# The three middle attention layers of a graph network as running sums by scans on VectorE, with rows gathered by position

## The reference, cut to what matters

```python
xs = (h @ Ws).reshape(N, H, C)
alpha_s = jnp.sum(xs * a_s, axis=-1);  alpha_d = jnp.sum(xd * a_d, axis=-1)
e = leaky_relu(alpha_s[src] + alpha_d[dst], 0.2)
ex = jnp.exp(e - segment_max(e, dst)[dst])
alpha = ex / (segment_sum(ex, dst)[dst] + 1e-16)
out = segment_sum(xs[src] * alpha[:, :, None], dst).reshape(N, H * C) + bias
```

## Time and profile before

| what | value |
|---|---|
| median of 3 runs | 10667.48 us (10661.7 to 10689.28) |
| the profiled execution's own time | 10696.05 us |
| its span, first to last instruction | 10694.3 us |
| PE / PEld / DVE busy | 5622.2 / 3714.7 / 4834.9 us |
| ACT / POOL busy | 1790.8 / 6522.5 us |
| gathers of the first network (912) | 426.4 to 1876.8 us of the span |
| gathers of the three middle layers (896 each) | 2068.0 to 3473.6, 3605.2 to 4999.7, 5107.8 to 6485.2 us |
| MLP over the edges, sum by source, end | about 6608 to 8610, 8896 to 10480, to 10694 us |

### The profile page before, as it was taken

One profiled execution on the slowest core, in us unless ns is written; L12 is line 12 of the kernel. 1 busy time (PEld: TensorE's weight loads), 2 busy tenths in 40 slices (PEclk: granted clock), 3 DMA queues, 4 the chain that ended last, 5 costly groups with the idle time before them and its releaser, 6 DMA issues. The chain is left out here.

```text
span 10694.3 us, 107517 instructions
## 1 busy us (share of the span) xinstructions
PE 5622.2 (53%) x22192; PEld 3714.7 (35%) x22192; DVE 4834.9 (45%) x11928; ACT 1790.8 (17%) x4846; POOL 6522.5 (61%) x6001
## 2 busy tenths in 40 slices
PE   6387878233333433334233334888888885333332
PEld 5133333133333333323233233444444443333332
DVE  6398989433332222222222223556565534444443
ACT  1211111211111100001000002333333331000002
POOL 2466666466666566665666665555555526888885
PEclk8688888566656556556555556999999986555555
DMA  1432324322223122222222223333333313444445
GB/s 67 120 59 56 58 56 56 78 44 46 43 45 45 38 44 46 45 45 41 45 45 46 46 46 69 88 86 91 89 92 85 90 30 31 36 36 36 36 36 95
DMA packets 705533, 611.82 MB, mean 57 GB/s; under 512 B 392917, under 2 KB 587604, under 8 KB 704308
## 3 DMA queue, kind: packets, MB, share of 16 engines
q0 software_dynamic: 332784, 513.58, 26.3%
q1 hardware_dynamic: 372676, 97.46, 4.3%
HBM read 483.12 MB, written 126.04 MB: 57 GB/s over the span
## 5 line engine op out<-in xcount | busy, mean ns | idle before, releaser
L899 POOL DMA_INDIRECT big<-table_layer,rec_L x2688 | 2658.9, 989 | 1598.8 <-issue 845.5
L970 PE MATMUL sums_L<-h,ident 128*128 128x128 f32 (+1 forms) x5376 | 1606.3, 465 | 720.7 <-DVE h L1068 301.9
L974 PE MATMUL sums_L<-carry_L,ident 128*128 128x128 f32 (+1 forms) x1792 | 679.5, 473 | 2172.6 <-DVE carry_L L1077 1438.6
L1077 DVE TENSOR_TENSOR carry_L<-sums_L,shrink_L 128x128 f32<-128x128 f32 (+1 forms) x896 | 348.1, 389 | 2841.9 <-remote 2222.7
L2061 POOL DMA_INDIRECT sums_by_source<-msg,to x896 | 1420.9, 1586 | 286.7 <-issue 227.6
L970 PEld LDWEIGHTS sums_L<-h,ident 128*128 128x128 f32 x5376 | 1092.2, 277 | 1200.3 <-issue 1175.0
L899 POOL DMA_INDIRECT big<-table_layer,idx_L x912 | 946.1, 1037 | 538.4 <-issue 307.2
L974 PEld LDWEIGHTS sums_L<-carry_L,ident 128*128 128x128 f32 x1792 | 395.2, 265 | 2359.7 <-DVE carry_L L1077 1497.4
L1611 POOL DMA_INDIRECT big<-table_layer,rec_m x900 | 859.2, 955 | 274.3 <-issue 274.3
L1661 PE MATMUL ps<-big,w 128*128 128x512 f32 x1792 | 833.5, 608 | 0.0
L924 ACT ACTIVATE big<-run_z_L 128x4 f32 (+1 forms) x900 | 194.6, 216 | 3554.4 <-DVE carry_L L1077 2257.0
(11 more groups left out here) (376 smaller groups left out, 8664.9 us busy)
## 6 DMA issues: line engine op xcount, KB each, us to landing
big<-table_layer,rec_L POOLq DMA_INDIRECT x2688
big<-table_layer,idx_L POOLq DMA_INDIRECT x912
table_layer<-xr SPq DMA_DIRECT2D x49, 296.0 KB
big<-table_layer,rec_m POOLq DMA_INDIRECT x900
sums_by_source<-msg,to POOLq DMA_INDIRECT x896
sums_by_source<-big SPq DMA_DIRECT2D x4, 3200.0 KB
q<-sums_by_source SPq DMA_DIRECT2D x28, 448.0 KB, 6.3
own_L<-own_layer SPq DMA_DIRECT2D x672, 2.0 KB
```

The costliest lines, as they stand in the source:

```text
L899: G.indirect_dma_start(out=g[b][:, u, s, :], out_offset=None, in_=table, in_offset=bass.IndirectOffsetOnAxis(ap=at, axis=0)).then_inc(gath ...
L970: PE.matmul(sums[b][u][:, 0:T * D], ident[:, :], prod[PROD[u]][:, s, :], start=(s == 0), stop=False, skip_group_check=True)
L974: PE.matmul(sums[b][u][:, 0:T * D], ident[:, :], carry[u % 2][:, :], start=False, stop=True, skip_group_check=True).then_inc(summed, 1)
L1077: V.tensor_tensor(carry[u % 2][:, :].rearrange("p (l c) -> p l c", c=C), before[:, 0:T * D].rearrange("p (l c) -> p l c", c=C), bc(shrink[ ...
```

## The change

- **Middle layers.** `attention` is used for the first network only. A new function `gat` does a middle layer. Its two buffers (`ring`, `RB` = 2) hold 16 slots each. A slot is an element of a running sum, with no items' sums and no PE: DVE makes the 4 products of a batch transposed (`prod`, channels outside, slots inside; the sources are read with a stride of 132 words), and then one scan over 4 x 33 x 17 = 2244 elements multiplies the running sum by `shrink` and adds `prod`. ACT expands the 64 fade values to 2112 with one exponential, and copies for each of the 4 items the element after its last slot into the accumulator.
- The own part of the score comes from PE: a one-hot of tile numbers against `own1T`, the transposed own scores, in place of SP's four small fetches.
- SP fetches for each batch the source positions (64 bytes a partition) and the tile numbers and lifts. It does so after the batch before in this buffer has been kept by ACT.
- **By position.** Tables hold rows by the node's place in the order. `onward` writes them with plain DMAs from SP, in place of POOL's scatters. The places are put into a spare column of the first network's table, come back with its gathers, and ACT and SP store them (`posb`, `pos_d`) for later layers and the MLP.
- Turns of the counting part are 26 in place of 25.

```diff
-            attention(f"L1{l}", 1, tab1_d[l], own1, acc1, g1, *scratch(1), ...)
+            gat(l, count if l == 0 else None)
```

Outside `gat`:

```diff
                         for j in range(NT):
-                            pool.wait_ge(staged, j + 1)
-                            G.indirect_dma_start(out=table, out_offset=... nid[:, j:j + 1] ..., in_=st[j % STG][:, 0:width])
+                            sp.wait_ge(staged, j + 1)
+                            sp.dma_start(table[j * P:(j + 1) * P, :], st[j % STG][:, 0:width]).then_inc(rows_out[j % STG], 16)
...
+                    if j >= EARLY:
+                        A.activation(stage[j % STG][:, :, A0], rank[:, j:j + 1].to_broadcast([P, T4]), ACT.Copy)
...
+                        act.wait_ge(pos_out[b], i * 16 + 16)
+                        A.activation(posb[b][:, :].rearrange("p (u s) -> p u s", s=S), g[b][:, :, :, A0], ACT.Copy
+                                     ).then_inc(pos_ok[b], 1)
...
+                        sp.dma_start(pos_d[:, ds((i * U + b * B) * S, B * S)], posb[b][:, :]).then_inc(pos_out[b], 16)
```

More of the change, by code:

```diff
@@ L34 @@
 HSTEP = 16
-HTURNS = 25
-EC2 = HTURNS * 2 * HSTEP
+RB = 2
+HTURNS = 26
+EC2 = HTURNS * RB * HSTEP
+SLOTS = B * S
 STG = 4
-PADI = 2 * U + U
+PADI = 48
 RMAX = 160
@@ L428, in _ @@
             def _(dve):
+                for v in range(STG):
+                    last = V.memset(stage[v][:, :, A0:A0P], 0.0)
+                last.then_inc(pos_blank, 1)
                 dve.wait_ge(edges_in, 16)
@@ L838, in attention @@
                 kept = sem(f"sums_kept_{tag}")
[L839 to L843, removed]
-                    counted = [sem(f"source_counted{b}") for b in range(2)]
-                    hist_ok = sem("sources_counted")
-                    histp = pb(f"histp_{tag}", [P, 512], fp32, ph)
                 NREC = 3 if T > 1 else 1
@@ L881, in _ @@
                         for b in range(2):
-                            fetch(i, b)
-                    if ahead:
-                        fetch(n, 0)
-                    if blank is not None:
-                        sp.wait_ge(zeroed, 16 * S)
+                            fetch(i + 1, b)
+                            store(i, b)
+                    for b in range(2):
+                        sp.wait_ge(own_in[b], n * 16 * B + 16 * B)
+                        sp.sem_inc(gate_s, 1)
+                        sp.wait_ge(pos_out[b], n * 16 + 16)
+                        sp.sem_inc(gate_s, 1)
                 @block.gpsimd
@@ L926, in keep @@
                                      ACT.Copy).then_inc(kept, 1)
+                    for b in range(2):
+                        act.sem_inc(pos_ok[b], 1)
                     act.sem_inc(kept, 2 * B)
@@ L956, in _, with turn @@
                 def _(pe):
[L957 removed]
+                    def turn(i):
                         for b in range(2):
@@ L962, in turn @@
                                 pe.wait_ge(kept, (i * 2 + b) * B + u + 2 + 2 * B - NB)
-                                if counting and u == 0:
-                                    pe.wait_ge(onehot[b], i + 1)
-                                    for t in range(HSTEP):
-                                        last = PE.matmul(histp[:, 0:NT], oneL[b][:, :, t], oneH[b][:, :, t],
-                                                         start=False, stop=False)
-                                    last.then_inc(counted[b], 1)
                                 for s in range(S):
@@ L978, in _ @@
                     n = turns(pe)
[L979 to L991 removed]
+                    with pe.Fori(0, n) as i:
+                        turn(i)
                 @block.vector
@@ L1544, in gnn @@
                 off = [sb(f"off{v}", [P, S], bf16, ph) for v in range(2)]
+                frm = [sb(f"from{u}", [P, S], i32, ph) for u in range(U)]
                 gx, ge, eT, h0, h1, h2, at = [], [], [], [], [[], []], [], 0
```

416 lines of the change are left out of this document (310 added, 106 removed).

## The result

| | before | changed | ratio, 95% interval |
|---|---|---|---|
| medians of 20 runs each | 10667.67 us | 10717.73 us | 1.0045 (1.0035 to 1.0054) |
| profiled execution, span | 10694.3 us | 10716.4 us | |

The changed kernel is slower by 50 us, 0.45%. The forecast was slower by 140 us. The sign and the likeliest mechanism were right.

A forecast was written before the change was run, and what follows sets the result against it. Middle layers were taken as bound by POOL's gather issue plus slow-sequencer waits. Loops +190, start -46, tables -17, preamble +8, first network +5 gave +140 us; less 28.6 for the profiled execution, 10808 us, 1.3% slower, range 10080 to 11130.

The forecast's parts named there:

- The gathers, products and the scan: Middle layers: bare gathers 20.0 us a batch, four products of 1.08 us each, one scan of 4.8 us.
- What DVE does to POOL: Middle layers: DVE instructions with two SBUF operands hold POOL, 4.2 us a batch for the scan, 1.3 for products.
- The chain that frees a buffer: Middle layers: last gather through keep and next fetch takes 22.2 us, covered by POOL's 25.5 us for the other batch.
- The crawl after the change: Middle layers: sequencers and semaphores slow during POOL's long gather bursts with register loads; 0.5 us a batch allowed.
- First middle layer's start: First middle layer: both first fetches stand ahead of SP's zeros, so gathers start earlier; gain 46 us.
- Tables by SP's plain DMAs: Between stages: SP writes four tables in place of POOL's scatters, PE and ACT needing nearly as much; net -17 us.
- The small terms: Outside the middle layers: preamble +8 us, first network +5, MLP 0.
- D: Rival, 0.10: in middle layers POOL's holds and its present waits cancel; 24.9 to 25.2 us a batch, 10640 to 10670 us.
- B: Rival, 0.31: the scan doesn't hold POOL in middle layers; 21.1 to 23.5 us a batch, 10052 to 10388 us.
- C: Rival, 0.17 with what lies above: slow register loads lengthen ACT's keep; 28.5 to 29 us a batch, 11228 to 11310 us.

The follow-up runs named there:

- shrink_psum: Changed kernel with shrink in PSUM, so the long scan has one SBUF operand instead of two; 10167.77 us, 0.9646 of before.
- ring_of_4: Changed kernel with RB = 4 in place of 2, and 13 counting turns of 4 batches in place of 26 of 2; 10626.74 us.
- set 3: Kernels run on one shared chip; the kernel before took 9521.85 us, the changed one 10259.81 us, ratio 1.0778.
- pool_scatters_2: Changed kernel with the four tables again written by POOL's indirect DMAs instead of SP's plain DMAs; 10865.97 us, 1.0148 of before.
- psum_weights_ring4_3: Changed kernel with shrink and a second copy of the weights in PSUM, and RB = 4; 0.9708 of before; the same kernel as psum_weights_ring4, there 0.9764.
- Sets 2 and 5: Two groups of runs: kernel before 9531.53 and 10559.04 us, changed kernel 1.0758 and 1.0099 of it.

## Where the prediction was right, and where it was wrong

*The gathers, products and the scan* were right. The products took 1.065 us (forecast 1.08), the scan 4.83 (4.8).

*What DVE does to POOL* was right in kind, and shrink_psum shows it by taking the second operand away. Its size was 5.7 us a batch against 5.5: some 4.3 us for the scan (forecast 4.2), 1.4 for the products and, in the first layer, the count's instructions (forecast 1.3 for the products alone). I let a gather ask at a random point of the scan. It doesn't: the gather beside the last product ends with it (2646.19 and 2646.34 us), so that in three of four batches the next one asks just after the scan has begun (0.06 us) and loses 4.57 us, and else 1.05 us into it and loses 3.60. That the mean of the two lies so near the mean of a random point is luck.

*The chain that frees a buffer* was rightly called covered (ring_of_4). *The crawl after the change*, 0.5 us a batch, was not there; 0.35 us of other pauses stood in its place. Small errors cancel: 26.0 forecast, 26.1 measured, +190 and +207 us.

*First middle layer's start*, -46 us, was right for the first gather (46.4), but I left out what is given back when POOL has used its 32 gathers and the third fetch is behind the zeros: I wrote that down, and didn't price it. Net some -33 to -36.

*Tables by SP's plain DMAs*, -17 us, is the step that failed. It priced the table between the first two middle layers by its one long scatter alone, and said that "in the other two PE and ACT need nearly as much" as the scatters. No row stood behind it. Between the stages the changed kernel gained 158.6 us, and 46.4 of them are the start; so the term is -112 us, not -17 (-99 by the traces of set 3). By table it is -16, -39, -38 and -19 where I had -5, -8, -1 and -3. ACT and PE stood waiting for POOL's scatters, and ran a tile in 0.71 us once SP wrote them. I had taken the waits of two engines in a chain for their work. The earlier trace rows could have told me: 49 scatters of 0.967 us with pauses of 0.30 are 62 us of the 70 that the third table took, and ACT had 29 us of work there. That the writer is the cause is shown by pool_scatters_2, which gives the scatters back to POOL in the changed kernel and takes 142 us more. This is some 30 us more than the whole term; the rest of what the change puts between the stages, such as the transposes of `own1`, would cost about that much the other way, and no run separates it.

The traces differ by +22 us where +140 was forecast. The tables make 95 us of these 118. The small terms (preamble, first network, MLP and what follows) were -26 together where I had +13, which makes 39; the loops give 17 the other way. In set 3 the two kernels' first networks and MLPs lie within 3.1 us of each other, so most of the -26 is the difference of two executions and no effect of the change. In the medians it is made up by the 28 us by which the trace of before lay over its own: 207 - 46 - 112 is +49, where the medians differ by 50.

Two smaller slips: the scatters' starts span 77.8 and 69.5 us in the second and third table, where I had 78.9 and 70.5 with the last scatter's own time; and D's 24.9 to 25.2 us a batch are 10622 to 10672 us by its own sum, not 10640 to 10670.

*Rivals.* B, the other side, gave 21.1 to 23.5 us a batch and 10052 to 10388 us if the scan doesn't hold POOL: shrink_psum built that case, with 23.0 to 23.6 us a batch and 0.9646 of before, which of the result's 10668 us would be 10290. C, the crawl on the serial chain, came only once the holds were gone (psum_weights_ring4_3). D's mechanism didn't happen, though the time ended not far from it.

*What the prediction didn't know* is that its baseline isn't one number. It took 4.9 us a batch of crawl in before as given. In sets 2 and 3 there is none, and the same change costs 7.6 and 7.8%: where the crawl is there, the holds that the change adds are largely paid for by the waits that it removes. So a forecast near the measured time is in part a matter of the set that it was measured in.

What stays open: what the crawl is, and why some sets have none. Sets 2 and 5 are recorded under the same chip number, one without it and one with it, so if that number names one chip, the chip alone doesn't decide. Why the changed kernel's loops never crawl is not known either; that POOL is stopped by a hold every 13 gathers or so is a guess.

## What to carry to other kernels

Beside a stream of indirect DMAs from POOL count a long DVE instruction with two SBUF operands at nearly its full length (4.3 of 4.83 us here) and short ones at less (1.3 of 4.3 us), and put one operand in PSUM where ACT writes it anyway. With four buffers beside it, that turned 25.9 us a batch into 20.1 in the sets without the crawl and into 23.3 with it, and made of a kernel 0.2 to 7.8% slower than before one of 0.971 to 0.977 of it (psum_weights_ring4). Before calling an engine the pace of a pipeline, subtract its waits: 28 us of ACT's work had been read as 70. And where the cost that a change removes comes from an effect that comes and goes, give the change two prices.

## What the runs showed of the hardware that was not expected

- The same kernel took 9522 to 9532 us in two sets and 10546 to 10705 us in four. The difference lies where sequencers work beside POOL's indirect DMAs: 4.1 us a batch in before's middle layers, some 400 us in the MLP and 79 in the preamble and the first network.
- The crawl doesn't need register loads. With them POOL waited 3.2 us a batch for late positions; without them it hardly waited, but its own gathers lasted 1.6 us a batch longer.
- A scan with one operand in PSUM, over a stretch of 2244 words, takes the same 4.83 us as with both in SBUF, and ACT's exponential of 2112 into PSUM 1.91 to 1.92 us against 1.95 into SBUF.
- Scans and gathers fall in step: of 165 gathers that began during a scan, 123 began within 0.1 us of its start and 42 at 1.05 us, none at another point.
